# Motif terms computed for two slabs of rows at a time, and the next image's statistics moved into the grams

## The reference

```python
patches = stack of the 9 shifts of feature          # (B, G=16, 9, Cg=8, L)
gram = einsum('bgjcl,bgjdl->bgjcd', motif, motif)
d2 = sq[..., :, None] + sq[..., None, :] - 2.0 * gram   # own distance = inf
nn_idx = argmin(d2)
u_max = max(nn_idx)
c_max = count of nn_idx == u_max
motif_nn = motif of channel u_max
term = floor(motif * motif_nn * c_max / Cg)
out_ser = motif * batch_mask + term                  # the mask is 0 for image 0, 1 for image 1
out = the 9 shifts added back in place               # (B, C, H, W)
```

## Time and profile before

| what | value |
|---|---|
| time, median of 3 runs | 1730.22 us (1729.72 to 1731.77) |
| time of the profiled execution | 1728.85 us |
| its span | 1727.1 us |
| TensorE busy | 1491.0 us, 86% |
| VectorE busy | 945.4 us, 55% |
| ScalarE busy | 732.5 us, 42% |
| GpSimd busy | 274.6 us, 16% |
| mean granted TensorE clock | 0.940 of full speed |

### The profile page before, as it was taken

How to read it: one execution, slowest core, us unless ns; L and a number is a source line. 1 busy time by engine, 2 the same in 40 slices (tenths; PEclk the granted TensorE clock), 3 DMA queues, 4 the chain that set the end, 5 groups by cost and what they waited for, 6 DMA issues and landing times. The chain is left out here.

```text
span 1727.1 us, 40359 instructions
## 1 busy us (share of the span) xinstructions
PE 1491.0 (86%) x16959; PEld 1252.2 (73%) x16959; DVE 945.4 (55%) x1525; ACT 732.5 (42%) x763; POOL 274.6 (16%) x250
## 2 busy tenths in 40 slices
PE   0899999699599588887959999988995994888998
PEld 0799999699599344444539999988995992444554
DVE  7333332123543489999962333321335425999998
ACT  0223232100254378877822232320004534878886
POOL 1422222000131111020022222220002202021100
PEclk9999999899799699999979999998997997999999
DMA  5211111011003364472122222200110215462511
GB/s 196 40 35 34 37 33 33 13 44 71 38 3 148 144 224 145 157 237 74 45 69 65 59 59 62 61 21 14 76 39 38 92 58 208 137 216 73 173 59 54
DMA packets 50958, 145.98 MB, mean 85 GB/s; under 512 B 12311, under 2 KB 33421, under 8 KB 48143
## 3 DMA queue, kind: packets, MB, share of 16 engines
q1 hardware_dynamic: 46192, 116.10, 20.9%
q0 software_dynamic: 4608, 27.49, 4.8%
HBM read 72.69 MB, written 37.75 MB: 64 GB/s over the span
## 5 line engine op out<-in xcount | busy, mean ns | idle before, releaser
L1307 PE MATMUL acc<-rnd,ident 128*128 128x376 f32 x1152 | 402.8, 494 | 25.8 <-ACT rnd L1290 25.8
L614 PE MATMUL ps_a<-wa,xa 128*128 128x192 f16 x2304 | 405.2, 247 | 9.0 <-DMA xc<-low 9.0
L615 PE MATMUL ps_a<-wb,xb 128*128 128x192 f16 x2304 | 404.6, 247 | 0.0
L1307 PEld LDWEIGHTS acc<-rnd,ident 128*128 128x128 f32 x1152 | 222.5, 197 | 152.1 <-ACT rnd L1290 27.2
L1285 ACT ACTIVATE rnd_m<-prod,plus_round,scale 128x1504 f32<-128x1504 f32 x144 | 236.0, 1639 | 119.5 <-DVE prod L1107 113.4
L1107 DVE TENSOR_TENSOR prod<-fc,near 128x1504 f32<-128x1504 f32 x144 | 246.8, 1714 | 38.6 <-DMA near<-near 21.2
L1219 DVE SCALAR_TENSOR_TENSOR over<-prod,scale,rnd 128x1504 bf16<-128x1504 f32 x144 | 255.6, 1777 | 2.0 <-PE acc L1311 1.9
L1290 ACT ACTIVATE rnd<-rnd_m,minus_round 128x1504 f32<-128x1504 f32 x144 | 223.1, 1550 | 26.4 <-PE acc L1311 21.3
L614 PEld LDWEIGHTS ps_a<-wa,xa 128*128 128x128 f16 x2304 | 226.5, 98 | 10.5 <-issue 8.5
L483 DVE TENSOR_TENSOR qk<-ps_a,qk 128x384 f16<-128x384 f32 x128 | 71.4, 558 | 293.8 <-ACT squares L564 293.8
L615 PEld LDWEIGHTS ps_a<-wb,xb 128*128 128x128 f16 x2304 | 226.9, 98 | 1.0
(11 more groups left out here) (222 smaller groups left out, 1911.1 us busy)
## 6 DMA issues: line engine op xcount, KB each, us to landing
x_planes<-img SPq DMA_DIRECT2D x8, 1536.0 KB, 5.6
f_planes<-img SPq DMA_DIRECT2D x8, 1536.0 KB, 11.3
fc<-f_planes SPq DMA_DIRECT2D x16, 768.0 KB, 8.0
x1c<-x_planes SPq DMA_DIRECT2D x16, 768.0 KB, 7.3
out<-x1c SPq DMA_DIRECT2D x16, 768.0 KB, 5.5
near<-near SPq DMA_DIRECT2D x96, 107.9 KB, 2.2
xb<-xa SPq DMA_DIRECT2D x64, 97.5 KB, 2.1
img<-in_x SPq DMA_DIRECT2D x4, 1536.0 KB, 12.8
```

Of the source, the lines that this page charges most:

```text
L614: nc.tensor.matmul(out, xa[:, row, dx:dx + W], wa[:, t, :], start=(t == 0), stop=False)
L615: nc.tensor.matmul(out, xb[:, row, dx:dx + W], wb[:, t, :], start=False, stop=False)
L1307: nc.tensor.matmul(o(m), k["ident"][:, :], rnd[:, n % RNDS, BR * m:BR * m + BR, :], start=False, stop=False, skip_group_check=True)
```

## The change

A step now holds both slabs of a pair and one tap: 36 steps an image, with `prod`, `rnd` and `over` of 3008 elements a partition. VectorE and ScalarE use one instruction where they had two; TensorE has as many as before. ScalarE's two roundings share one buffer. `PRODS` is 2 steps, and the over lags by one step, so the queue of VectorE is product n, over n-1. At the first tap of a pair, both finishes of the pair before follow the over. The moves of both slabs are issued together when the product of the step before is done, and one semaphore counts them. The loads of `fc` and `x1c`, the stores and the gathers are issued in pairs, at other taps. In `motif_grams`, VectorE takes 2 or 3 of the next image's statistics after each unit, from an `x_next` of one quarter, which SyncE loads whole; its queue does this ahead of the writes of `f_planes`. `motif_terms` has no statistics any more.

```diff
+            def load_next(q):
+                if x_after is not None:
+                    if q > 0:
+                        sp.wait_ge(next_stats, q)
+                    sp.dma_start(x_next[:], x_after[:, QROWS * q:QROWS * q + QROWS, :]).then_inc(next_in, 16)
+            for q in range(NQ):
+                load_next(q)
...
+            def next_share(u):
+                q, first = u // PER_CHUNK, GN * (u % PER_CHUNK) // PER_CHUNK
+                if x_after is not None:
+                    if u % PER_CHUNK == 0:
+                        dve.wait_ge(next_in, 16 * (q + 1))
+                    last = chunk_stats(nc, x_next, 0, k["stats"], q, range(first, GN * (u % PER_CHUNK + 1) // PER_CHUNK))
+                    if u % PER_CHUNK == PER_CHUNK - 1:
+                        last.then_inc(next_stats, 1)
...
                 out(u)
+                next_share(u)
...
-    PRODS, RNDS = 4, 3
+    PRODS, RNDS = 2, 3
...
-        prod = sb("prod", [P, PRODS, R, WM], F32)
-        rnd_m = sb("rnd_m", [P, 2, R, WM], F32)
-        rnd = sb("rnd", [P, RNDS, R, WM], F32)
-        over = sb("over", [P, 2, R, WM], BF16)
-        if b + 1 < B:
-            x_next = sb("x_next", [P, 2 * QROWS, C], F32)
-            next_in = [sem(f"next_in{j}_") for j in range(2)]
-            next_stats = sem("next_stats")
+        prod = sb("prod", [P, PRODS, 2, R, WM], F32)
+        rnd = sb("rnd", [P, RNDS, 2, R, WM], F32)
+        over = sb("over", [P, 2, 2, R, WM], BF16)
...
+        moved = sem("moved")
+        steps = [(m, sh) for m in range(N // 2) for sh in range(KK)]
...
+                pair = (2 * m, 2 * m + 1)
                 if sh >= 1:
                     if sh == 1:
+                        for i in pair:
+                            sp.wait_ge(near2_in[i % SLOTS], 16 * (i // SLOTS + 1))
+                    sp.wait_ge(prod_done, n)
+                    for i in pair:
+                        sp.dma_start(near[MC - sh:P:MC, i % SLOTS, run(i)], near2[MC - sh:P:MC, i % SLOTS, run(i)]
+                                     ).then_inc(moved, 16)
+                if sh == 2 and m == 0:
+                    for i in pair:
+                        load_rows(x1c, x1_dram, i, x1_in)
+                if sh == 3 and m >= 1:
+                    for i in pair:
+                        store(i - 2)
+                if sh == 5 and 2 * m + 2 < N:
+                    for i in pair:
+                        if m >= 1 and b == 1:
                             sp.wait_ge(fold, i - 1)
+                        load_rows(fc, f_dram, i + 2, fc_in)
+                if sh == 7 and 2 * m + 2 < N:
+                    for i in pair:
+                        if m >= 1:
+                            sp.wait_ge(stored[(i + 2) % SLOTS], 16 * ((i + 2) // SLOTS))
+                        load_rows(x1c, x1_dram, i + 2, x1_in)
...
+            for m in range(N // 2 - 1):
+                for sh, second in ((1, 0), (3, 1)):
+                    pool.wait_ge(prod_done, KK * m + sh)
+                    for i in (2 * m + 2, 2 * m + 3):
+                        if i == N - 1 and second == 0:
+                            nc.gpsimd.memset(near[:, i % SLOTS, R * C:NR * C], 0.0).then_inc(edged, 1)
+                        gather(i, second)
...
+            def make(n):
+                m, sh = steps[n]
+                if sh == 0:
+                    for i in (2 * m, 2 * m + 1):
+                        dve.wait_ge(near_in[i % SLOTS], 16 * (i // SLOTS + 1))
+                        dve.wait_ge(fc_in[i % SLOTS], 16 * (i // SLOTS + 1))
+                    dve.wait_ge(edged, 2 if m == N // 2 - 1 else 1)
+                else:
+                    dve.wait_ge(moved, 32 * (8 * m + sh))
+                if n >= PRODS:
+                    dve.wait_ge(over_done, n - PRODS + 1)
+                product(nc.vector, n).then_inc(prod_done, 1)
             def overshoot(n):
                 sh = steps[n][1]
                 dve.wait_ge(rnd_done, n + 1)
                 if n >= 2:
+                    dve.wait_ge(acc_over, 2 * (n - 1))
+                nc.vector.scalar_tensor_tensor(flat(over[:, n % 2]), flat(prod[:, n % PRODS]), scale[:, sh:sh + 1],
+                                               flat(rnd[:, n % RNDS]), ALU.mult, ALU.is_lt).then_inc(over_done, 1)
             def finish(i):
+                dve.wait_ge(acc_over, 2 * KK * (i // 2 + 1) - 1 + i % 2)
...
+            for n, (m, sh) in enumerate(steps):
+                make(n)
+                if n >= 1:
+                    overshoot(n - 1)
+                if sh == 0 and m >= 1:
+                    finish(2 * m - 2)
+                    finish(2 * m - 1)
+                if b == 1 and sh in (4, 6):
+                    own_patches(2 * m + sh // 2 - 2)
+            overshoot(len(steps) - 1)
             finish(N - 2)
             finish(N - 1)
-            if b + 1 < B:
...
+            for n, (m, sh) in enumerate(steps):
+                act.wait_ge(prod_done, n + 1)
+                if n >= RNDS:
+                    act.wait_ge(acc_rnd, n - RNDS + 1)
+                    act.wait_ge(over_done, n - RNDS + 1)
+                r = flat(rnd[:, n % RNDS])
+                nc.scalar.activation(r, flat(prod[:, n % PRODS]), ACT.Identity, bias=k["plus_round"][:, 0:1],
+                                     scale=scale[:, sh:sh + 1]).then_inc(rm_done, 1)
                 act.wait_ge(rm_done, n + 1)
+                nc.scalar.activation(r, r, ACT.Identity, bias=k["minus_round"][:, 0:1]).then_inc(rnd_done, 1)
...
+            def place(s, m, dx):
+                return acc[s][:, m, 0:BR * C].rearrange("p (r c) -> p r c", c=C)[:, :, dx:dx + WM]
+            for n, (m, sh) in enumerate(steps):
                 dx = TAPS[sh][1]
+                for s in range(2):
+                    if sh == 0:
+                        if m >= 1:
+                            pe.wait_ge(out_ready, 2 * m - 1 + s)
+                        for j in range(R // BR):
+                            nc.tensor.matmul(acc[s][:, j, 0:BR * C], k["zeros"][:, 0:P], k["zeros"][:, 0:BR * C],
+                                             start=True, stop=False, skip_group_check=True)
+                    if s == 0:
+                        pe.wait_ge(rnd_done, n + 1)
+                    for j in range(R // BR):
+                        last = nc.tensor.matmul(place(s, j, dx), k["ident"][:, :],
+                                                rnd[:, n % RNDS, s, BR * j:BR * j + BR, :], start=False,
+                                                stop=False, skip_group_check=True)
+                last.then_inc(acc_rnd, 1)
                 pe.wait_ge(over_done, n + 1)
+                for s in range(2):
+                    for j in range(R // BR):
+                        last = nc.tensor.matmul(place(s, j, dx), k["minus_ident"][:, :],
+                                                over[:, n % 2, s, BR * j:BR * j + BR, :],
+                                                start=False, stop=(sh == KK - 1), skip_group_check=True)
+                    last.then_inc(acc_over, 1)
```

More of the change, by code:

```diff
@@ L750, in motif_grams @@
         turned_lo = [sb(f"turned_lo{s}_", [P, TCOLS + 8], F16) for s in range(2)]
+        x_next = sb("x_next", [P, QROWS, C], F32) if x_after is not None else None
         part = sb("m_part", [P, 4, GN], F32)
@@ L1082, in motif_terms @@
-        after = {i: number[(i, KK - 1)] + 1 for i in range(N)}
-        last_row = lambda i: min(R * i + R - 1, HM - 1)
-        def product_made(eng, n):
-            eng.wait_ge(prod_p if on_pool[n] else prod_v, sum(p == on_pool[n] for p in on_pool[:n + 1]))
-        def product_inputs(eng, n):
-            i, sh = steps[n]
-            s = i % SLOTS
-            if sh == 0:
-                eng.wait_ge(near_in[s], 16 * (i // SLOTS + 1))
-                eng.wait_ge(fc_in[s], 16 * (i // SLOTS + 1))
-                eng.wait_ge(edged, 2 if i == N - 1 else 1)
-            else:
-                eng.wait_ge(moved[i % 2], 16 * (8 * (i // 2) + sh))
-            if n >= PRODS:
-                eng.wait_ge(over_done, n - PRODS + 1)
+        moved = sem("moved")
@@ L1186, in _ @@
                 gather(1, second)
-            for n, (i, sh) in enumerate(steps):
-                if sh in (1, 3) and i + 2 < N:
-                    product_made(pool, n)
-                    if sh == 1 and i + 2 == N - 1:
-                        nc.gpsimd.memset(near[:, (i + 2) % SLOTS, R * C:NR * C], 0.0).then_inc(edged, 1)
-                    gather(i + 2, sh // 2)
-                if on_pool[n]:
-                    product_inputs(pool, n)
-                    product(nc.gpsimd, n).then_inc(prod_p, 1)
+            for m in range(N // 2 - 1):
[5 more added lines that the diff above has]
+                        gather(i, second)
         @block.vector
@@ L1305, in _ @@
-                pe.wait_ge(rnd_done, n + 1)
-                for m in range(R // BR):
```

(6 more changed lines are left out.)

111 lines of the change are left out of this document (16 added, 95 removed).

## The result

The changed kernel takes 1751.45 us (median of 4 runs, 1750.78 to 1754.66), the kernel before 1730.99 on the same chip: a ratio of 1.0123, with a 95% interval of 1.0109 to 1.0137. It is **slower by 1.2%**, some 20.5 us, outside the predicted range of 1712 to 1741. The profiled execution has a span of 1749.5 us, against 1727.1; the granted clock is 0.941 of full, against 0.940.

What follows compares the result with a forecast made beforehand. The prediction took VectorE to bound the terms. Image 1's terms -18.8 us, image 2's +10.1 and grams +1.5 gave -7.2 us, so 1723 us against a median of 1730.22, with a range of 1712 to 1741.

Steps and rivals of the forecast that it cites:

- Full steps: Terms, VectorE: doubled products and overs, with a wait on the over directly in front, save 5.3 us an image.
- End: End of each image's terms: last product's end to last finish's end grows from 10.7 to 15.1 us, +4.4 us.
- ScalarE and TensorE under it: Terms: ScalarE's roundings become 2.89 and 2.80 us and stay hidden, TensorE needs 6.32 of 6.56 us; no cost.
- Turns: Terms, change of pair: VectorE idles 1.9 us before the first finish, three times an image, +5.7 us.
- Start: Start of each image's terms: first product needs both slabs' gathers and second product waits for the moves, +2.5 us.
- Moves: Terms: late near<-near moves cost 7 us an image besides the start, -4.3 us in image 1, +2.8 in image 2.
- A: Rival: in terms the second move lands too late at every step and moves become the bound; 1731 to 1752 us, chance 0.23.
- Statistics: Image 1's terms: 128 bn_stats of 0.17 us each leave VectorE, the bound engine, -21.8 us.
- Grams: Image 1's grams: statistics fit VectorE's gaps, but loads of x_next cost 0.5 us at three places, +1.5 us.
- Rival D: Grams: loads of x_next landing after 6.5 to 7 us cost 6 to 8 us; 1728 to 1731 us, chance 0.12.
- B: Rival: in terms the wait on over costs nothing, 3.7 us less an image; 1716 us, chance 0.07.
- C: Rival: in terms the moves never come late, -14 us; 1709 us, chance 0.08.

Runs made afterwards that it cites:

- experiment 5: The changed kernel with three buffers of prod instead of two, so a product no longer waits for the over directly in front; 1744.88 us.
- experiment 11: The changed kernel with GpSimd's first gathers for pair 1 released by the second product instead of the first; 1743.51 us.
- experiment 1: The kernel before with only the statistics of image 2 moved into image 1's grams, terms still one slab a step; 1728.55 us, ratio 0.9993.
- 9: The kernel before, one slab a step, with image 2's statistics in image 1's grams, norm ahead, statistics in the first eight of twelve units; 1715.22 us.
- Experiments 3: The changed kernel with the norm of the next piece put ahead of the statistics; 1753.84 us, ratio 1.0133.
- 8: The changed kernel with the norm ahead of the statistics and four statistics after each of the first eight of twelve units, so x_next loads earlier; 1740.67 us.
- 12: The changed kernel with statistics in the first eight of twelve units and the earlier load, but the norm left behind the statistics; 1744.76 us.

## Why the prediction was wrong, point by point

The sum missed by 29.6 us (22.4 longer where 7.2 shorter was forecast): 13.5 in image 1's grams, 11.1 in its terms, 4.5 in image 2's terms and 0.5 between. To close the account, VectorE's time in the two stages of terms, in us: for every row of its timeline the time to the next start (the last one to its own end), less the idle time.

| VectorE in terms | image 1, before | after | image 2, before | after |
|---|---|---|---|---|
| products and overs | 240.1 | 238.9 | 241.1 | 237.4 |
| statistics | 22.0 | 0 | 0 | 0 |
| finishes, own patches | 13.5 | 13.4 | 29.3 | 29.1 |
| waits for moves | 14.0 | 18.0 | 7.2 | 17.4 |
| waits for first gathers | 8.9 | 11.3 | 8.6 | 9.7 |
| waits for TensorE, ScalarE | 2.1 | 10.9 | 4.0 | 10.8 |

- **Full steps, -5.3 each: half of it in image 1.** The table's row also holds the overs behind the last product, which the forecast puts under End. Up to the last product's end, as forecast, products and overs went from 235.0 to 232.3 us in image 1 (-2.7) and from 235.9 to 230.8 in image 2 (-5.1). A step that waits for its over gained nothing. The step "so 0.11 us more" failed: the earlier trace rows price the wait behind a short operation, and behind an over of 3008 elements it is 0.19 (experiment 5). I carried the row over to an operation nearly 12 times as long; 34 waits at 0.08 more are 2.7 us, about what image 1 lacks. That image 2's value is nearly the forecast is luck: eight of its overs stand in front of own_patches and are not waited for, which I had not counted, and before's products were 1.0 us dearer there. The value of 3.45 us lies inside my ends (twice 0.11).
- **ScalarE and TensorE under it: right.** 2.89 and 2.80 us as estimated; the only wait for rnd is at the end.
- **Turns (+5.7) and end (+4.4): right.** 1.87 us three times, and 15.2 us against 15.1.
- **Start, +2.5 each: half of it.** In image 2 the third one-slab product had started 15.65 us after index (1448.25 - 1432.6), the second doubled one now does 20.57 after: +4.9. "The second [...] lands 2.2 us later" failed. I took a move that runs alone; it landed after 5.9 (measured from index the moves went out 1.4 us sooner than I had put them, which hides part of it), since the same product's end also releases the next pair's gathers (experiment 11).
- **Moves, 7 us an image besides the start: too low.** 11.1 and 10.4 (18.0 - 6.9 and 17.4 - 7.0), nearly all at step 4, one of the four steps at which I had expected them in pair 0. I put 1.7 us there, and 1.5 in pairs 1 and 2; it is 3.0 to 4.5. There GpSimd's gathers, now 3.8 and 3.1 us an issue, and from pair 1 on the stores go out just before: the gathers issued from 1543.3 and 1547.4 landed after 10.4 us in the median, the moves behind them (1549.7 and 1550.3) after 5.1 and 6.2 with 3.45 of cover. The rows point to the gathers: pair 0 has no stores there and has the wait, pair 3 has the stores and no gathers, and there the moves landed after 2.2 us and nothing waited. At the other steps there is next to none: the 3.30 us of cover do suffice for a move by itself, and that part of the argument against A stood.
- **Statistics, -21.8 in image 1's terms: 9 us too much.** "All 128 lie on the bound engine" was true, but it wasn't bound all the time. Taking them out gave 12.4 us in experiment 1 and 13.0 in 9, because waits for moves took their place, 6.5 us in the one and 4.6 in the other, where 2.2 before overs and 0.6 before finishes joined them. I had only counted what the pairs do to the moves, not what the statistics had covered.
- **Grams, +1.5: wrong by 13.5 us, the largest miss.** The step "a transfer of 1536 KB lands after 5.0 us" failed; those it waits for landed after 6.4, 7.7 and 9.3. The earlier trace rows show the fastest of eight such transfers in before (5.0 to 6.9 us, median 5.6), and all eight are stores, while x_next is a load. In before a load of 768 KB (x1c, 1467.3) landed after 4.5 us and a store of that size (1720.2) after 3.2. And the norm, which I had put inside the wait at its 1.75 us, took 2.9 more: I had moved it by three statistics without looking at what GpSimd does then. Rival D (landings of 6.5 to 7 us, grams 6 to 8 longer, 0.12) named the mechanism, and even it was too small. Experiments 3, 8 and 12 account for the +15, load and norm together.
- **Rivals.** A's 1731 to 1752 holds the time, but its mechanism is not there. B and C are refuted: the wait on over costs more and not less, and moves are late. D's own time does not quite follow from the sum: 6 to 8 us in place of 1.5 give 1727.5 to 1729.5, not 1728 to 1731.
- **The last sign, TensorE at its half level after a turn:** it was there and cost VectorE nothing. Behind image 2's first turn the granted clock was 0.53 of full from 1541 to 1548, and VectorE worked through it (6.9 of 7.0 us); before had 0.51 from 1520.5 to 1527.

Five terms missed in the same direction (full steps in image 1, start, moves, statistics, grams). Three of them (start, moves, grams) took a landing from a quiet row, while the change brings transfers together; such misses don't cancel, and the range should have held them all at once. What was not tried: x_next in two buffers, and whether the loads' 9.3 us come from the f_planes stores behind them. In experiment 9, where the load is issued some 15 us sooner, the last one has them right behind as well (524.27) and took 8.1, so that stays open. Why the loads landed later than the stores of the earlier trace rows, and the last two later than the first two, is open too.

## What to carry to other kernels

Before work is taken off a busy engine, look at what it covers: its waits for transfers grow by part of what it gives back (22 us removed, 12 to 13 gained). Before work is put into another engine's gaps, check when its buffer comes free and what now stands behind it in the queue; the same 24 us of statistics cost 12 to 15 us when the load had no slack and nothing when it had four units and the norm stood ahead of them. And merging two operations into one of twice the size saves little where the pipeline loses its distance: the buffer count, the cover of each transfer and the handoffs at turns and end all change with the size of a step.

## What the runs showed of the hardware

- The cost of a wait on the instruction directly in front isn't a constant: 0.11 us behind a reduction of 256 elements (0.52 against 0.41), 0.19 behind an over of 3008 (3.45 against 3.26). The two differ in kind as well as in size, and nothing between them was measured.
- An instruction of the norm, about 0.5 us by itself, that starts behind a GpSimd subtraction's start lasts until that one ends: 3.4 us for one instruction, 4.6 instead of 1.75 for the four. Taking out the transposes (L966) beside such a subtraction keeps its time: three took 1.62 us at 486.57 in before.
- The issue of a gather on GpSimd goes with what VectorE runs. Beside an idle VectorE it takes 0.94 us, beside the one-slab operations 2.24, beside those of 3008 elements 3.1 and 3.8. No run changes VectorE's work alone, so that it is the cause is not shown. Before, then after, from the tile view of near:

```profile
L1176 POOL DMA_INDIRECT near<-f_planes,index x32: 937/2239/2244, 582.6 to 1607.7; - x32
```

```profile
L1163 POOL DMA_INDIRECT near<-f_planes,index x32: 933/2102/3805, 597.6 to 1619.2; - x32
```
